# Softplus widths and last additions spread over GpSimd, scan begun with two decays

## The chip, the cores and the metric

The kernel runs on one core of a Trainium2 chip. The metric is device time in microseconds for one execution, inputs and outputs in HBM. One core has TensorE (PE, matmuls into PSUM), VectorE (DVE), ScalarE (ACT), GpSimd (POOL) and SyncE (SP, here a DMA queue). Each runs its own instruction list in order; they meet through semaphores. GpSimd cannot reach PSUM.

## The reference

A network of four blocks on an image `[2, 32, 32, 32]`: each block adds a mixer and then a token network to `x`. Only the first mixer, `L0_conv`, a windowed selective scan, is touched. Cut to what matters:

```python
def _forward(x, ...):                        # B=2, C=32, D=64, 16 states, 4 scan orders, windows 8x8
    xv, z = split(x @ in_proj_w.T)
    xc = silu(depthwise_conv3x3(xv) + conv_b)
    xs = four scan orders of the windows of xc            # Hilbert order, its transpose, both reversed
    dts, Bs, Cs = split(einsum('bkdl,kcd->bkcl', xs, x_proj_w))
    dts = softplus(einsum('bkrl,kdr->bkdl', dts, dt_projs_w) + dt_projs_b)
    A = -exp(A_logs)
    def step(h, (u, dt, Bl, Cl)):
        h = h * exp(dt[..., None] * A) + (dt * u)[..., None] * Bl[:, :, None, :]
        return h, einsum('bkdn,bkn->bkd', h, Cl)
    ys = lax.scan(step, 0, ...)
    y = layernorm(ys + Ds * xs, summed over the four orders, back in image order)
    return (y * silu(z)) @ out_proj_w.T
```

`dt` is called `step` in the kernel and `dt * u` is called `drive`.

## The kernel before

The kernel is a list of blocks; a block begins when all engines have finished the one before. Four matter here.

**The block of tokens and sequences** (L350 to L409) turns the convolution's result into scan order, `seq` `[128, 2, 16, 128]`: 128 partitions hold direction and channel, then come order `k`, window and position, 2 x 2048 columns in all. VectorE and ScalarE copy it out of PSUM in turns.

**The softplus block** (L426 to L507) works on 8 chunks of 512 columns, `cols(i)`. TensorE makes the raw step width `p_d` (bank `i % 4`) and, for the first four chunks, the raw B and C rows `p_bc`. softplus(v) is log(1 + exp(-|v|)) + max(v, 0), made precise by what rounding lost of exp(-|v|) in 1 + exp(-|v|):

- ScalarE, per chunk: Abs (L446) into `ex`, Relu (L447) into `above`, Exp (L449), and for i < 4 the copy of `p_bc` to bf16 `part[0]` (L452). Then eight logarithms (L457) into `step` after a table load (L454), and a last table load (L458).
- VectorE, per chunk: "keep" (L466), (ex + 1) - 1 into `drive`; "lost" (L473), ex - drive; the addition of it to `above` (L481); for i < 4 the remainder of B and C, `rest` (L470), its bf16 cast `part[1]` (L476) and the second remainder `part[2]` (L484). Then, 1024 columns wide, step = step - ln_one + above (L495) four times and drive = step * seq (L489) twice.
- SP stacks the three parts under each other into `b_parts` and `c_parts` (96 rows) by 12 DMAs (L506), part by part, and the block ends when all have landed. GpSimd has nothing.
- TensorE streams 16 filler matmuls (`keep_streaming`, L95) after the first logarithm.

**The scan block** (L557 to L776) has 64 units `u`, each 1024 columns of one of 16 states; four groups of 16 units (`NS`), so group 0 is the first half of order k = 0. Per unit: TensorE spreads a B row over the partitions (L587, `p_bb`) and a C row (L593, `p_cb`); ScalarE makes the decays exp(step * A) (L658, `d_a`) and copies `p_cb` out (L664, `cb`); VectorE multiplies drive and B into `p_bb` (L711) and scans (L722, `hs`); GpSimd multiplies by C (L775, `hc`); TensorE sums over states (L562, `p_y`). In each fourth unit ("on GpSimd") B goes by way of L615, ScalarE's copy (L669) and GpSimd's product (L770) into `d_bu`, and the decays into `p_bb`. Buffers are rings of three (`RING`): VectorE's scan of unit u waits for `hc` of unit u - 3, GpSimd's `hc` of unit u for TensorE's sum of u - 3, and on TensorE the sum of u - 3 stands ahead of the spread for u + 1. GpSimd also makes drive = step * seq for order k = 1 in units 2 and 18 (L766).

**The tail** of the scan block normalises, gates and mixes (up to L757). After it come the other blocks of the network, which the change does not touch.

Of the kernel before, what the change touches and what calls it, by code (L numbers as in the profile page):

```python
# [17 lines left out]
R = NB * C  # L18
# [41 lines left out]
def build_program(nc, io):  # L60
    with ExitStack() as ctx:
# [153 lines left out]
        with ExitStack() as st:  # L215
# [15 lines left out]
            pick = sb("pick", [96, NS, 128], BF16, stack=st)  # L231
            tok = sb("tok", [L, NW, D], stack=st)
# [3 lines left out]
            with ExitStack() as s2:  # L236
# [13 lines left out]
                with ExitStack() as s3:  # L250
# [10 lines left out]
                    with nc.Block() as block:  # L261
# [11 lines left out]
                        def _(pool):  # L273
                            pool.memset(padded[:], 0.0).then_inc(sig["border_zero"], 1)
                            pool.memset(w_dt[:], 0.0)
                            pool.wait_ge(sig["load_in"], 64)
# [65 lines left out]
                with ExitStack() as s3:  # L342
# [4 lines left out]
                    ln_one = sb("ln_one", [128, 2], stack=s2)  # L347
                    with nc.Block() as block:
                        @block.gpsimd
                        def _(pool):  # L350

                            pool.tensor_copy(pick[:], pick_f)
                            pool.memset(ln_one[:], 0.0)
# [51 lines left out]
                        @block.scalar  # L405
                        def _(act):
                            for i in range(1, NPAIR, 2):
                                act.wait_ge(sig["seq_made"], i + 1)
                                copy_seq(i, act.copy).then_inc(sig["seq_copied_odd"], 1)  # L409


                with ExitStack() as s3:
                    p_bc = ps("p_bc", [128, 4, BANK], stack=s3)
                    p_d = ps("p_d", [128, 4, BANK], stack=s3)
                    part = [sb(f"part{i}", [128, NW * L], BF16, stack=s3) for i in range(3)]
                    rest = sb("rest", [128, NW * L], stack=s3)
                    above = sb("above", [128, 2, NW * L], stack=s3)
# [4 lines left out]
                    def wide(m):  # L422
                        return m // 2, slice((m % 2) * 2 * BANK, (m % 2 + 1) * 2 * BANK)
                    seqf = seq[:].rearrange("p k w l -> p k (w l)")
                    with nc.Block() as block:
                        @block.tensor  # L426
                        def _(pe):
                            for i in range(NCH):
                                k, c = cols(i)
                                if i >= 4:  # L430
                                    pe.wait_ge(sig["step_read"], i - 3)
# [5 lines left out]
                            pe.wait_ge(sig["log1"], 1)  # L437
                            keep_streaming(pe, p_d[:, 0], 16)

                        @block.scalar  # L440
                        def _(act):
                            act.activation(ln_one[:, 1:2], ln_one[:, 1:2], ACT.Exp)
                            for i in range(NCH):
# [3 lines left out]
                                act.activation(above[:, k, c], p_d[:, i % 4], ACT.Relu, bias=b_dt[:, k:k + 1]).then_inc(sig["step_read"], 1)  # L447
                                act.wait_ge(sig["abs"], i + 1)
                                act.activation(ex[:, k, c], ex[:, k, c], ACT.Exp, scale=-1.0).then_inc(sig["exp_neg"], 1)  # L449
                                if i < 4:  # L450
                                    act.wait_ge(sig["bc_made"], i + 1)
                                    act.activation(part[0][:, c], p_bc[:, i], ACT.Copy).then_inc(sig["part_hi"], 1)  # L452
                            act.wait_ge(sig["exp_neg"], NCH)
                            act.activation(ln_one[:, 0:1], ln_one[:, 0:1], ACT.Ln, bias=1.0)  # L454
# [2053 lines left out]
```

## Time and profile before

| | |
|---|---|
| median of 3 runs | 994.14 us (993.59 to 1001.52) |
| profiled execution | 993.03 us |
| its span in the trace | 991.2 us |
| softplus block, 36.6 to 67.4 | 30.8 us |
| scan block up to the tail, 67.4 to 277.0 | 209.6 us |
| tail, 277.0 to 294.7 | 17.7 us |
| the rest, after 294.7 | 696.5 us |

The span runs from the first to the last instruction of the trace; the 1.8 us beyond it are in the execution's time but not in the trace. A row of the timeline gives start, duration, engine, line, operation, output and input with their shapes, count, and in brackets how long the engine had been idle and what ended that. Rows of a merged group give the time from its first start to its last end.

### The profile page before, as it was taken

The page shows a single profiled execution, that of the slowest core. Times are in us where ns is not written, and L with a number is a line of the kernel's source. Part 1 is how long each engine was busy: PE and PEld are TensorE (multiplying, and loading weights), DVE is VectorE, ACT ScalarE, POOL GpSimd, SP SyncE. Part 2 cuts the span into 40 slices and gives each one's busy share as a digit, 9 for nine tenths or more (in the row PEclk, how much of TensorE's full clock was granted, in tenths as well). Part 3 has the DMA queues.
Part 4 walks back from the last instruction along what each step waited for, and adds up shares of the span by engine and source line. Part 5 has one row for each costly group of instructions (what it writes and reads, how often), then busy time and mean ns, then how long its engine had stood idle before and what let it go on. Part 6 is the DMA issues. An engine that isn't in the chain of part 4 may idle for free. (4 is left out here: it accounts for less than half of the span.)

```text
span 991.2 us, 15215 instructions
## 1 busy us (share of the span) xinstructions
PE 893.9 (90%) x6134; PEld 514.5 (52%) x6134; DVE 418.7 (42%) x715; ACT 450.7 (45%) x1491; POOL 230.5 (23%) x140
## 2 busy tenths in 40 slices
PE   7848888888986877999999999999999999999986
PEld 4416767767753443344444444445555544554543
DVE  4599999999965554600000000002004500202763
ACT  4667777777635533243333333333333333334642
POOL 3209999899830000020000000000000000000410
PEclk9978999999996588799999999999999999999987
DMA  3020000000000001110000000000000000000000
GB/s 80 15 50 1 1 1 2 1 1 1 1 3 4 1 1 33 46 36 1 2 1 1 1 1 2 1 1 1 1 1 1 1 1 1 1 1 2 1 24 11
DMA packets 10319, 8.28 MB, mean 8 GB/s; under 512 B 7346, under 2 KB 8610, under 8 KB 10152
## 3 DMA queue, kind: packets, MB, share of 16 engines
q1 hardware_dynamic: 10248, 7.31, 2.9%
q8 instruction: 48, 0.79, 0.3%
q14 instruction: 23, 0.19, 0.1%
HBM read 5.47 MB, written 0.26 MB: 6 GB/s over the span
## 5 line engine op out<-in xcount | busy, mean ns | idle before, releaser
L890 PE MATMUL L2p_z<-stream 128*128 128x512 bf16 x943 | 366.7, 390 | 0.0
L932 ACT ACTIVATE L2yx<-L2p_z 32x2 f32<-32x2 f32 x1024 | 165.0, 161 | 323.3 <-PE L2p_z L909 323.2
L909 PEld LDWEIGHTS L2p_z<-L2yx,L2v 64*32 64x32 f32 x2048 | 137.6, 104 | 224.7 <-ACT L2yx L932 218.5
L909 PE MATMUL L2p_z<-L2yx,L2v 64*32 64x2 f32 x2048 | 225.5, 178 | 1.0 <-PEq L810 0.9
L775 POOL TENSOR_TENSOR hc<-hs,cb 128x1024 f32<-128x1024 f32 x64 | 149.5, 2358 | 10.7 <-DVE hs L722 10.7
L562 PEld LDWEIGHTS p_y<-ident,hc 128*128 128x128 f32 x1024 | 125.7, 194 | 10.8 <-POOL hc L775 1.5
L1588 DVE COPY xn<-L2yx 32x512 f32<-32x512 f32 (+1 forms) x2 | 0.8, 384 | 302.7 <-ACT L2yx L932 302.7
L562 PE MATMUL p_y<-ident,hc 128*128 128x128 f32 x1024 | 126.3, 277 | 0.3 <-POOL hc L775 0.3
L1588 POOL COPY xn<-L2yx 32x128 f32<-32x128 f32 x1 | 0.3, 283 | 484.2 <-SPq L1931 484.2
L722 DVE TENSOR_TENSOR_SCAN hs<-d_a,p_bb 128x1024 f32<-128x1024 f32 x48 | 109.7, 2286 | 6.8 <-ACT d_a L658 0.8
L890 PEld LDWEIGHTS L2p_z<-stream 128*128 128x128 bf16 x943 | 90.1, 96 | 15.1
L664 ACT ACTIVATE cb<-p_cb 128x1024 f32<-128x1024 f32 x64 | 65.2, 1019 | 13.0 <-PE p_cb L593 12.1
L658 ACT ACTIVATE d_a<-step,decay 128x1016 f32<-128x1016 f32 x48 | 54.6, 1138 | 18.5 <-DVE hs L722 11.6
L711 DVE TENSOR_TENSOR p_bb<-drive,p_bb 128x1024 f32<-128x1024 f32 x48 | 58.0, 1209 | 2.7 <-PE p_bb L587 2.6
L593 PE MATMUL p_cb<-c_parts,pick 96*128 96x512 bf16 x128 | 40.4, 399 | 12.3 <-ACT d_bu L669 10.5
L587 PE MATMUL p_bb<-b_parts,pick 96*128 96x512 bf16 x96 | 30.5, 400 | 12.7 <-DVE hs L722 6.3
L770 POOL TENSOR_TENSOR d_bu<-drive,d_bu 128x1024 f32<-128x1024 f32 x16 | 37.9, 2369 | 10.2 <-ACT d_bu L669 10.2
L982 PE MATMUL L0p_z<-L0yx,L0v 64*32 64x64 f32 x192 | 30.4, 306 | 10.0 <-PEq L810 4.5
L722 DVE TENSOR_TENSOR_SCAN hs<-p_bb,d_bu 128x1024 f32<-128x1024 f32 x16 | 36.3, 2266 | 0.7 <-ACT p_bb L658 0.7
L982 PEld LDWEIGHTS L0p_z<-L0yx,L0v 64*32 64x32 f32 x192 | 17.5, 139 | 22.5 <-ACT L0yx L1002 16.2
L593 PEld LDWEIGHTS p_cb<-c_parts,pick 96*128 96x128 bf16 x128 | 10.9, 99 | 31.3 <-ACT d_bu L669 18.8
L1002 ACT ACTIVATE L0yx<-L0p_z 32x64 f32<-32x64 f32 x96 | 20.1, 214 | 13.3 <-PE L0p_z L982 12.9
(509 smaller groups left out, 849.5 us busy)
## 6 DMA issues: line engine op xcount, KB each, us to landing
y_l<-in_pick SPq DMA_DIRECT2D x1, 768.0 KB
b_parts<-part SPq DMA_DIRECT2D x6, 128.0 KB, 2.3
c_parts<-part SPq DMA_DIRECT2D x6, 128.0 KB, 2.3
pos<-in_pos SPq DMA_DIRECT2D x1, 512.0 KB, 3.6
ao<-in_at_o SPq DMA_DIRECT2D x1, 512.0 KB, 3.9
L1w<-in_L_w SPq DMA_DIRECT2D x1, 297.0 KB
L3w<-in_L_w SPq DMA_DIRECT2D x1, 297.0 KB
x_tok<-in_x SPq DMA_DIRECT2D x2, 128.0 KB, 3.0
```

The costliest lines, as they stand in the source:

```text
L562: last = pe.matmul(p_y[:, j], hc[:, v % RING, j * L:(j + 1) * L], ident[:], start=False, stop=(v % NS == NS - 1 and j % 4 == 3))
L593: last = pe.matmul(p_cb[:, h * BANK:(h + 1) * BANK], pick[:, n], c_parts[:, k, c], start=True, stop=True)
L658: act.activation(dst[:, :, 1:L], src[:, :, 1:L], ACT.Exp, scale=decay[:, k, n:n + 1]).then_inc(sig["d_a"], 1)
L664: act.activation(cb[:, u % RING], p_cb[:], ACT.Copy).then_inc(sig["p_cb_read"], 1)
L711: dve.tensor_tensor(p_bb[:, u % 2], drive[:, k, c0:c0 + UC], p_bb[:, u % 2], ALU.mult).then_inc(sig["d_bu"], 1)
L722: dve.tensor_tensor_scan(hs[:, u % RING], decays, inputs, 0.0, ALU.mult, ALU.add).then_inc(sig["scanned"], 1)
L770: pool.tensor_tensor(d_bu_of(u), drive[:, k, c0:c0 + UC], d_bu_of(u), ALU.mult).then_inc(sig["d_bu_pool"], 1)
L775: pool.tensor_tensor(hc[:, u % RING], hs[:, u % RING], cb[:, u % RING], ALU.mult).then_inc(sig["hc"], 1)
L890: pe.matmul(p_z[:, 1, 0:each], stream[:, 0:128], stream[:, 0:each], start=True, stop=True)
L909: pe.matmul(p_step[:, t % 2], v[:, 0:C], yx[:, NB * t:NB * (t + 1)], start=True, stop=True).then_inc(s("preact"), 1)
L932: act.activation(yx[0:C, NB * (t + 1):NB * (t + 2)], p_step[:, t % 2], ACT.Sigmoid).then_inc(s("state"), 1)
L982: pe.matmul(p_z[0:C, f, 0:NB * n], v[:, 0:C], by_batch[:, cols], start=True, stop=True).then_inc(s("preact"), 1)
```

## The change

- Four buffers, `part`, `above`, `ln_one` (now three columns) and a constant `one`, live through the scan; `y_tok` and `y_sq` reuse `conv` and `tok`.
- The logarithm of one, its negative and a first exponential move to ScalarE's list in the block of tokens and sequences.
- Softplus block: VectorE makes max(v, 0) of chunks 0 to 3, by TENSOR_SCALAR from PSUM; ScalarE keeps Relu for chunks 4 to 7. "Keep" becomes a SCALAR_TENSOR_TENSOR with a broadcast column. `part[1]` comes straight from `p_bc` by a second subtraction, not by a cast. "Lost" (8) and `part[2]` (4) and the additions of chunks 4 to 7 go to GpSimd; VectorE keeps the additions of chunks 0 to 3, with ln_one in them. Only the first 1024 columns are finished in this block (one addition, one product).
- The other three quarters are finished in the scan block: the second by VectorE's addition ahead of unit 0 and GpSimd's product in unit 0; the third and fourth by ScalarE's subtraction of ln_one in units 2 and 18, GpSimd's addition in units 4 and 20 and its product in units 6 and 22 (before: 2 and 18).
- The parts are stacked by 18 DMAs in three pieces; TensorE waits for each at units 0, 16 and 32, and the softplus block no longer waits for their landing.
- 26 filler matmuls instead of 16, from the last exponential on, and 4 in each of units 0 to 2.
- ScalarE makes the decays of units 0 and 1 ahead of its first copy.

```diff
                         def _(pe):
                             for i in range(NCH):
                                 if i >= 4:
-                                    pe.wait_ge(sig["step_read"], i - 3)
+                                    pe.wait_ge(sig["abs"], i - 3)
+                                    pe.wait_ge(sig["positive_early"], i - 3)
...
-                            pe.wait_ge(sig["log1"], 1)
-                            keep_streaming(pe, p_d[:, 0], 16)
+                            pe.wait_ge(sig["exp_neg"], NCH)
+                            keep_streaming(pe, p_d[:, 0], 26)
...
                         @block.vector
                         def _(dve):
...
+                            def keep(i):
+                                k, c = cols(i)
+                                dve.wait_ge(sig["exp_neg"], i + 1)
+                                dve.scalar_tensor_tensor(drive[:, k, c], ex[:, k, c], 1.0, one[:].broadcast_to([128, BANK]), ALU.add, ALU.subtract).then_inc(sig["kept"], 1)
+
+                            def add_lost(i):
+                                k, c = cols(i)
+                                dve.wait_ge(sig["lost"], i + 1)
+                                dve.scalar_tensor_tensor(above[:, k, c], above[:, k, c], ln_one[:, 0:1], drive[:, k, c], ALU.subtract, ALU.add).then_inc(sig["with_max"], 1)
+
+                            for i in range(4):
+                                k, c = cols(i)
+                                dve.wait_ge(sig["abs"], i + 1)
+                                dve.tensor_scalar(above[:, k, c], p_d[:, i], b_dt[:, k:k + 1], 0.0, ALU.add, ALU.max).then_inc(sig["positive_early"], 1)
+                                if i:
+                                    keep(i - 1)
+                                dve.wait_ge(sig["part_hi"], i + 1)
+                                dve.tensor_tensor(part[1][:, c], p_bc[:, i], part[0][:, c], ALU.subtract)
+                                dve.tensor_tensor(rest[:, c], p_bc[:, i], part[0][:, c], ALU.subtract).then_inc(sig["rest"], 1)
+                                if i >= 2:
+                                    dve.wait_ge(sig["positive_early"], i - 1)
+                                    add_lost(i - 2)
+                            for i in range(3, NCH):
+                                keep(i)
+                                if i < 5:
+                                    add_lost(i - 1)
...
+                            dve.tensor_tensor(step[:, k, c], step[:, k, c], above[:, k, c], ALU.add).then_inc(sig["softplus"], 1)
+                            dve.wait_ge(sig["softplus"], 1)
+                            dve.tensor_tensor(drive[:, k, c], step[:, k, c], seqf[:, k, c], ALU.mult)
+
+                        @block.gpsimd
+                        def _(pool):
+                            for i in range(NCH):
+                                k, c = cols(i)
+                                pool.wait_ge(sig["kept"], i + 1)
+                                pool.tensor_tensor(drive[:, k, c], ex[:, k, c], drive[:, k, c], ALU.subtract).then_inc(sig["lost"], 1)
+                                if i < 4:
+                                    pool.wait_ge(sig["rest"], i + 1)
+                                    pool.tensor_tensor(part[2][:, c], rest[:, c], part[1][:, c], ALU.subtract).then_inc(sig["part_lo"], 1)
+                                else:
+                                    pool.wait_ge(sig["lost"], i + 1)
+                                    pool.tensor_tensor(above[:, k, c], above[:, k, c], drive[:, k, c], ALU.add)
...
+                            stack("parts_of_0", 2, 0, slice(0, 2 * BANK))
+                            stack("parts_of_1", 4, 0, slice(2 * BANK, 4 * BANK))
+                            stack("parts_of_2", 4, 1, slice(0, 4 * BANK))
...
+                                if u < RING:
+                                    keep_streaming(pe, p_y[:, 0:4].rearrange("p w d -> p (w d)"), 4)
...
+                            if u == 0:
+                                decays(0)
+                                decays(1)
+                            elif u >= 2:
+                                decays(u)
...
+                            if u in (2, 2 + NS):
+                                c = slice(u // NS * UC, (u // NS + 1) * UC)
+                                act.activation(step[:, 1, c], step[:, 1, c], ACT.Identity, bias=ln_one[:, 2:3]).then_inc(sig["late_log"], 1)
...
+                        second = slice(UC, 2 * UC)
+                        dve.tensor_tensor(step[:, 0, second], step[:, 0, second], above[:, 0, second], ALU.add).then_inc(sig["softplus"], 1)
...
-                            if u in (2, 2 + NS):
-                                c = slice(u // NS * UC, (u // NS + 1) * UC)
+                            if u == 0:
+                                c = slice(UC, 2 * UC)
+                                pool.wait_ge(sig["softplus"], 2)
+                                pool.tensor_tensor(drive[:, 0, c], step[:, 0, c], seqf[:, 0, c], ALU.mult)
+                            c = slice(u // NS * UC, (u // NS + 1) * UC)
+                            if u in (4, 4 + NS):
+                                pool.wait_ge(sig["late_log"], u // NS + 1)
+                                pool.tensor_tensor(step[:, 1, c], step[:, 1, c], above[:, 1, c], ALU.add).then_inc(sig["late_step"], 1)
+                            if u in (6, 6 + NS):
+                                pool.wait_ge(sig["late_step"], u // NS + 1)
                                 pool.tensor_tensor(drive[:, 1, c], step[:, 1, c], seqf[:, 1, c], ALU.mult)
```

## Rows read from the trace of the kernel before

**Rows 1.** The page: busy time, share of the span and instructions of each engine.
```profile
PE 893.9 (90%) x6134; PEld 514.5 (52%) x6134; DVE 418.7 (42%) x715; ACT 450.7 (45%) x1491; POOL 230.5 (23%) x140
```

**Rows 2.** Windows by stage: length, busy of PE, PEld, DVE, ACT, POOL; clock; DMA.
```profile
36.60:67.40 30.80, 17.52 (x48) 5.41 (x48) 26.14 (x42) 23.96 (x42) 0.00 (x0) 0.87 0.23 52
67.40:277.00 209.60, 184.32 (x1296) 145.91 (x1297) 199.64 (x113) 153.65 (x169) 188.64 (x82) 0.96 0.00 1
294.70:991.20 696.50, 650.33 (x4461) 335.67 (x4461) 166.63 (x517) 254.84 (x1247) 26.63 (x32) 0.93 0.02 6
```

**Rows 3.** Timeline of the softplus block: first and last of TensorE and ScalarE.
```profile
36.64 1.10 PE L432 MATMUL p_d<-seq,w_dt 128*128 128x512 f32 x2 [0.94 <-PEq L348]
38.68 1.12 PE L432 MATMUL p_d<-seq,w_dt 128*128 128x512 f32 x2
38.01 0.67 ACT L446 ACTIVATE ex<-p_d,b_dt 128x512 f32<-128x512 f32 x1
59.13 1.28 ACT L458 ACT_TABLE_LOAD   x1
```

**Rows 4.** Groups of instructions: line, engine, shapes, count | busy us, mean ns | idle.
```profile
L466 DVE TENSOR_SCALAR drive<-ex 128x512 f32<-128x512 f32 x8 | 3.4, 420 | 5.2 <-ACT ex L449 5.2
L470 DVE TENSOR_TENSOR rest<-p_bc,part 128x512 f32<-128x512 f32 x4 | 2.7, 681 | 0.0
L489 DVE TENSOR_TENSOR drive<-step,seq 128x1024 f32<-128x1024 f32 x2 | 2.4, 1218 | 0.0
```

**Rows 5.** GpSimd alone, groups with shapes kept apart.
```profile
L775 POOL TENSOR_TENSOR hc<-hs,cb 128x1024 f32<-128x1024 f32 x64 | 149.5, 2358 | 10.7 <-DVE hs L722 10.7
L355 POOL TENSOR_TENSOR skip<-skip 128x128 f32<-128x128 f32 x1 | 0.4, 449 | 0.0
```

**Rows 6.** Attention stage: timeline rows, and durations min/median/max of two lines.
```profile
L1555 DVE TENSOR_TENSOR scored<-scored,anmx x8: 1224/1225/2782, 749.6 to 927.5; 128x1024 f32<-128x1024 f32 x8
927.50 2.78 DVE L1555 TENSOR_TENSOR scored<-scored,anmx 128x1024 f32<-128x1024 f32 x1
942.04 1.26 DVE L2094 SCALAR_TENSOR_TENSOR sc<-sc,pos 128x128 f32<-128x128 f32 x1
925.38 3.82 POOL L2267 TENSOR_TENSOR prod<-e 128x1024 f32<-128x1024 f32 x2 [9.84 <-DVE e L1786]
L2273 POOL TENSOR_TENSOR prod<-e x8: 293/298/1279, 929.2 to 931.9; 128x64 f32<-128x64 f32 x8
940.30 2.85 POOL L2280 TENSOR_TENSOR pv<-sc,e 128x1024 f32<-128x1024 f32 x1 [2.35 <-ACT sc L2221]
```

**Rows 7.** Timeline of the start of the scan block: GpSimd, then VectorE.
```profile
67.41 0.12 POOL L762 MEMSET d_a<- 128x16 f32 x1 [35.89 <-POOLq L425]
68.49 1.23 DVE L711 TENSOR_TENSOR p_bb<-drive,p_bb 128x1024 f32<-128x1024 f32 x1 [1.37 <-PE p_bb L587]
72.35 1.23 DVE L711 TENSOR_TENSOR p_bb<-drive,p_bb 128x1024 f32<-128x1024 f32 x1 [0.24 <-PE p_bb L587]
79.40 2.26 DVE L722 TENSOR_TENSOR_SCAN hs<-p_bb,d_bu 128x1024 f32<-128x1024 f32 x1
```

**Rows 8.** Timeline of VectorE: two scans of the on-GpSimd kind, units 11 and 15.
```profile
105.14 2.26 DVE L722 TENSOR_TENSOR_SCAN hs<-p_bb,d_bu 128x1024 f32<-128x1024 f32 x1
117.95 2.26 DVE L722 TENSOR_TENSOR_SCAN hs<-p_bb,d_bu 128x1024 f32<-128x1024 f32 x1
```

**Rows 9.** Timeline of GpSimd in the scan: its first pauses.
```profile
105.30 4.68 POOL L775 TENSOR_TENSOR hc<-hs,cb 128x1024 f32<-128x1024 f32 x2 [0.23 <-DVE hs L722]
118.11 4.68 POOL L775 TENSOR_TENSOR hc<-hs,cb 128x1024 f32<-128x1024 f32 x2 [1.16 <-DVE hs L722]
```

**Rows 10.** Windows of 2 us, columns as in Rows 2; TensorE's clock after POOL.
```profile
53.00:55.00 2.00, 0.00 (x0) 0.00 (x0) 1.97 (x5) 1.97 (x4) 0.00 (x0) 0.50 0.32 74
59.00:61.00 2.00, 2.00 (x9) 0.71 (x7) 1.96 (x3) 1.60 (x3) 0.00 (x0) 0.86 0.15 33
77.00:79.00 2.00, 2.00 (x7) 1.08 (x7) 1.90 (x2) 1.95 (x2) 2.00 (x2) 0.50 0.00 0
```

More of the change, by code:

```diff
@@ L231, in build_program @@
             pick = sb("pick", [96, NS, 128], BF16, stack=st)
+            part = [sb(f"part{i}", [128, NW * L], BF16, stack=st) for i in range(3)]
+            above = sb("above", [128, 2, NW * L], stack=st)
+            ln_one = sb("ln_one", [128, 3], stack=st)
+            one = sb("one", [128, 1], stack=st)
             tok = sb("tok", [L, NW, D], stack=st)
@@ L275, in _ @@
                             pool.memset(w_dt[:], 0.0)
+                            pool.memset(ln_one[:], 0.0)
+                            pool.memset(one[:], 1.0)
                             pool.wait_ge(sig["load_in"], 64)
@@ L452, in _ @@
                                     act.activation(part[0][:, c], p_bc[:, i], ACT.Copy).then_inc(sig["part_hi"], 1)
+                                else:
+                                    act.activation(above[:, k, c], p_d[:, i % 4], ACT.Relu, bias=b_dt[:, k:k + 1])
+                                act.wait_ge(sig["abs"], i + 1)
+                                act.activation(ex[:, k, c], ex[:, k, c], ACT.Exp, scale=-1.0).then_inc(sig["exp_neg"], 1)
                             act.wait_ge(sig["exp_neg"], NCH)
-                            act.activation(ln_one[:, 0:1], ln_one[:, 0:1], ACT.Ln, bias=1.0)
                             for i in range(NCH):
@@ L500, in _, with stack @@
                         @block.sync
                         def _(sp):
-                            for i, s in enumerate(("part_hi", "part_mid", "part_lo")):
-                                sp.wait_ge(sig[s], 4)
-                                for k in range(2):
+                            def stack(name, chunks, k, c):
+                                for i, s in enumerate(("part_hi", "rest", "part_lo")):
+                                    sp.wait_ge(sig[s], chunks)
                                     for dst, row in ((b_parts, 0), (c_parts, 32)):
-                                        sp.dma_start(dst[32 * i:32 * i + 32, k], part[i][k * R + row:k * R + row + 32]).then_inc(sig["parts_stacked"], 16)
@@ L645, in read_y, with decays @@
                             act.copy(group_out(g, 0, HW8), group_in(0, HW8)).then_inc(sig["y_read"], 1)
-                        act.wait_ge(sig["first_decay_zero"], 1)
-                        for u in range(NU):
+                        def decays(u):
                             k, c0, n = unit(u)
+                            if u == NS:
+                                act.wait_ge(sig["softplus"], 2)
+                            if u in (2 * NS, 3 * NS):
+                                act.wait_ge(sig["late_step"], u // NS - 1)
                             if u >= 2:
@@ L696, in _ @@
                         for i, w in enumerate((0, 4)):
[L697 to L698 removed]
+                            act.wait_ge(sig["y_summed"], NU + i)
+                            act.copy(group_out(3, w, 4), group_in(w, 4)).then_inc(sig["y_read"], 1)
                         squares(1)
```

70 lines of the change are left out of this document (18 added, 52 removed).

## The prediction

> **What bounds the kernel now.** I read the page's busy times first [rows 1]: TensorE leads with 90%, but that is a sum over stages and partly filler, so it says little about this change. The table by stage [rows 2] shows where the edits live: a softplus stage of 30.8 us (36.60 to 67.40), the scan of 209.6 us, 17.7 us of tail, and 696.5 us in which no line is touched. Within the stages I then read the timeline.
>
> *Softplus stage.* ScalarE's chunk work begins at 38.01 and its last table load at 59.13 [rows 3]; the next block begins only at 67.41 [rows 7]. In between only VectorE works (26.14 of 30.8 us busy, with a late start); GpSimd does nothing (0.00) [rows 2]. VectorE ends the stage.
>
> *Scan stage.* VectorE is busy 199.64 of 209.6 us, GpSimd 188.64, ScalarE 153.65 [rows 2]. Per four units VectorE needs three products and four scans: 3 x 3.54 + 2.20 = 12.8 us, what lies between two scans of the on-GpSimd kind [rows 8]. GpSimd needs four `hc` and one `d_bu` at a spacing of 2.33 us (two in 4.68) = 11.7 us [rows 9]. So VectorE sets the scan, with GpSimd 1.1 us behind it per four units. GpSimd is the one to watch: its first pause once started, of 0.23 us, comes at 105.30, 37.9 us into the block, and only at 118.11 does it show the steady gap of 1.16 us [rows 9].
>
> **The change, part by part.**
>
> *Start of the stage.* The first table load (1.28) and a 0.20 exponential move to the block before, where ScalarE has idle time. But the first `p_d` matmul ends at 37.74 and Abs began at 38.01 [rows 3]: 0.2 us won, no more.
>
> *ScalarE.* Four Relu go to VectorE. TensorE's repeat of `p_d` and `p_bc` is 2.06 us (36.64, 38.68) [rows 3], so three ScalarE passes per chunk (about 1.6 us) now wait for it, where four took as long as TensorE. Exponentials end near 52.7 instead of 53.4, logarithms near 58.4, the last table load near 59.7. ScalarE alone would end the block near 60.
>
> *VectorE.* 8 keeps grow from 0.42 (TENSOR_SCALAR) to about 0.69 (two-input form); 4 positives (0.69), 8 part differences (0.68) and 4 additions (0.69) are its own; then one 1024-wide addition and one product (1.22 each) [rows 4]. That is 24 passes at a spacing near 0.61 plus 2.4: about 17 us from 38.5, done near 57 if nobody holds it up.
>
> *GpSimd* gets 16 passes of 128x512. No such shape is in the trace: 128x128 takes 449 ns, 128x1024 takes 2358 [rows 5]; so on a line between them 1.27, a spacing of 1.24 like the 2.33 for 2.36. The first can start when the first keep is done: Abs, copy and Exp of chunk 0 end near 39.95, the second positive is ahead of the keep on VectorE, so near 42.0. Sixteen passes: 42.0 + 19.8 = 61.8, a few waits for keeps: 62.3. Other 1024-wide forms give bounds: 3.82 for two, and 2.85 [rows 6]; half of each is 0.96 and 1.42, so 15.3 to 22.7 us for the sixteen.
>
> *The port.* Whether these passes run beside VectorE's decides the case. In the attention stage a VectorE TENSOR_TENSOR of 1024 with both inputs in SBUF takes 1.22 seven times and 2.78 once (min and median against max) [rows 6]. The long one began at 927.50 while GpSimd's second product (3.82 for two from 925.38) ran until 929.20; 929.2 - 927.5 + 1.2 is 2.9. Of GpSimd's next eight passes, from 929.2, one took 1279 ns where the others took 298 [rows 6]: it waited for VectorE. Once more: a SCALAR_TENSOR_TENSOR of only 128 columns at 942.04 took 1.26, and ended 0.15 us behind the GpSimd pass of 2.85 that had begun at 940.30 [rows 6]. The scans do not show it: one of their two inputs is in PSUM. So I take it that a VectorE pass with two SBUF inputs and a GpSimd pass exclude each other wholly.
> The Trainium skill, "SBUF — State Buffer", section "Who interferes with whom", says this of just these operand kinds, and that `tensor_scalar` in its fast form excludes GpSimd too, so that the new form of the keep would free nothing. By that rule the sum is the same 999; without it, rival B's. The trace agrees for the two-input passes (2.78 against 1.22) and shows no fast form beside GpSimd.
>
> After 42.0 VectorE has 7 keeps and 4 additions (11 x 0.65 = 7.2) and two wide passes (2.4) with both inputs in SBUF. These 9.6 us do not fit under GpSimd's 19.8: 42.0 + 19.8 + 7.2 + 2.4 = 71.4. In the long pass above the pair overlapped by about 0.14, so some of it comes back; waits for keeps cost some. I take 71.0 for the end, 71.3 for the next block, against 67.41: **+3.9 us**. With the bounds of the GpSimd pass: +0.4 to +6.8.
>
> *DMAs in pieces.* 18 issues on SP's queue replace 12; I put one at 0.6 us, and twice that would change nothing. Pieces of the first half need `part_lo` of two chunks (near 48.4), the last eight follow the fourth near 56.7, landing near 64. Only unit 0's pieces must be there at 71.3: nothing. If the port is no obstacle, the fourth is at 52.3 and all has landed near 60, still ahead of 62.6.
>
> *Clock.* TensorE falls to 0.5 (1.2 GHz) once idle since 48.6, is back at full (2.4 GHz) near 59.5, when filler had run since 55.5, and is still at 0.5 at 77 to 79 after idling from 61 to 67 [rows 10]. 26 fillers instead of 16, from 52.7: ten at 0.43 and sixteen at 0.21, done near 60.4. With 11 us idle behind them the scan again begins at 1.2 GHz.
>
> *Scan start* (relative to the block's start; before: products 0 and 1 at 1.08 and 4.94, scan 3 at 11.99 [rows 7]). VectorE first adds for 1.22: product 0 at 1.35, scan 0 at 2.7. On TensorE four fillers (1.7 at this clock) stand ahead of unit 3's B spread, and ScalarE's copy comes after two decays: that spread starts at 3.6 instead of 3.0, product 1 at 5.5, scan 1 at 6.85. Again for unit 2 (fillers after the spread of unit 1): scan 2 near 10.7, scan 3 near 12.95. So 0.95 later.
>
> *GpSimd in the scan.* Three more passes net: product in unit 0, additions in units 4 and 20; the products of 2 and 18 move to 6 and 22. Queued behind are `d_bu`, then all `hc`; VectorE waits for `hc` three units back, TensorE sums them ahead of the next B spread. Chained at 2.33: unit 7's `hc` ends at 34.1 after the start (before, 30.7), unit 8's at 38.7, exactly when scan 11 wants it, and the spread for unit 12 is 0.15 late. Once more after units 20 and 22. Together 0.3 us; the bound is both additions whole, 4.7. ScalarE's two subtractions (1.1 each) lie in its slack. The tail keeps its work; the reused buffers cost nothing.
>
> *Sum.* Profiled execution: 993.03 (span 991.2 and 1.8 around it); +3.9 + 0.95 + 0.15 = +5.0, so 998.0. The median of the runs is 994.14, 1.1 more: **999 us**.
>
> **Rivals.**
> *A. The port excludes, and lengths are as taken*: 999; own range 994.5 (short passes -3.5, scan start early -1.0) to 1003.5 (long ones +2.9 and waits +1.6, or the waits alone near their bound). Chance 0.70.
> *B. No exclusion for 512-wide passes.* GpSimd ends the block at 62.3, next block 62.6: -4.8, TensorE idle for only 2.2 us, so at full clock, scan start +0.2, ties +0.3: 994.1 - 4.3 = 990. For it: the scans' GpSimd spacing of 2.33 is unhurt by VectorE. Against it: the three long passes of [rows 6]. 0.10. This is the faster side; it decides as soon as VectorE's 9.6 us run beneath.
> *C. The gain and the loss cancel.* GpSimd passes as short as the 3.82-for-two form: +0.4 in place of +3.9, the rest as above: 995.5. Against it: that form reads other operands, and 82 passes of the plain one take 2.36. 0.10.
> *D. GpSimd becomes the bound of the scan.* If VectorE inherits all three added passes (7.0) on top of 3.9 and 0.95: 994.1 + 11.9 = 1006. For it: no pause before 105.30 already now [rows 9]. Against it: the slack of 1.1 per four units. It decides from 5 us of such waits on. 0.10.
>
> A run of this kernel tells about 1% (9.9 us) from no change. A and C lie within; B too. Slower: D and the edge of A, 0.11. Faster: B with a further gain, 0.03. Same: 0.86. The range leaves out B and D: 992 to 1004.
>
> **What would show it.** In the softplus stage GpSimd should be busy from 42 to 71 with mean passes well over 1.27, and VectorE's 512-wide two-SBUF passes between 0.69 and 1.9; PSUM-fed ones stay at 0.68. The scan block should start near 71.3 at clock 0.5. First scan 2.7 behind it; scan 11 to 12 with a gap under 0.5; scan spacing later unchanged. If GpSimd's passes stay at 1.27 with VectorE's at 0.69, B holds. If scans in units 8 to 15 are spaced over 3.6, D holds. I would be wrong outright if the later stages moved, 696.5 us that I take as fixed, for instance by the clock's falls coming elsewhere.

## The result, and the profile after

| | before | after |
|---|---|---|
| median | 994.43 us (20 runs, 990.52 to 1001.98) | 1000.15 us (20 runs, 997.03 to 1009.35) |
| ratio | | 1.0053, 95% interval 1.0037 to 1.0069 |
| profiled execution / span | 993.03 / 991.2 us | 1000.17 / 998.4 us |
| scan block begins at | 67.41 | 69.37 |
| last of the 64 scans begins at | 274.53 | 279.90 |
| next block begins at | 294.71 | 300.73 |

The changed kernel is slower by half a per cent, 5.3 us by the ratio. 999 us with no change beyond 1% was forecast. Of the 7.2 us between the two spans, 1.96 arise in the softplus block, 3.41 in the scan, 0.65 in the tail and 1.2 in blocks that the change does not touch. This is a sum over one profiled execution of each kernel; the 5.3 us are over 20 runs of each.

The busy times of the page, against [rows 1]: GpSimd has 32.1 us more, and VectorE has 1.9 more, not less.

```profile
PE 899.9 (90%) x6156; PEld 518.8 (52%) x6156; DVE 420.6 (42%) x700; ACT 451.8 (45%) x1491; POOL 262.6 (26%) x160
```

The same stages as in [rows 2], by window (length, then busy time of PE, PEld, DVE, ACT, POOL; clock; DMA):

```profile
36.60:69.36 32.76, 19.59 (x58) 6.19 (x58) 26.55 (x26) 20.78 (x35) 24.69 (x16) 0.85 0.21 49
69.36:282.00 212.64, 185.86 (x1304) 147.13 (x1305) 200.74 (x113) 154.76 (x171) 195.66 (x85) 0.97 0.00 1
282.00:300.70 18.70, 15.56 (x125) 9.99 (x123) 10.77 (x17) 4.85 (x10) 2.72 (x2) 0.91 0.00 1
300.70:998.40 697.70, 650.75 (x4461) 336.96 (x4461) 166.62 (x517) 254.81 (x1247) 26.63 (x32) 0.93 0.02 6
```

VectorE's busy time in the softplus stage did not shrink (26.55 against 26.14), though it does 26 passes where it did 42. GpSimd is busy for 24.69 us with 16 passes: 1.54 each.

The groups of that stage, VectorE's against [rows 4] (in each: line, engine, operation, shapes, count, busy us, mean ns, idle time before):

```profile
L505 POOL TENSOR_TENSOR drive<-ex,drive 128x512 f32<-128x512 f32 x8 | 12.5, 1558 | 12.4 <-DVE drive L470 12.4
L511 POOL TENSOR_TENSOR above<-above,drive 128x512 f32<-128x512 f32 x4 | 6.6, 1645 | 0.3
L508 POOL TENSOR_TENSOR part<-rest,part 128x512 bf16<-128x512 f32 x4 | 6.0, 1497 | 0.0
L470 DVE SCALAR_TENSOR_TENSOR drive<-ex,one 128x512 f32<-128x512 f32 x8 | 11.4, 1445 | 0.0
L484 DVE TENSOR_TENSOR part<-p_bc,part 128x512 bf16<-128x512 f32 x4 | 2.7, 682 | 0.2 <-ACT part L454 0.2
L496 DVE TENSOR_TENSOR step<-step,above 128x1024 f32<-128x1024 f32 x1 | 2.3, 2278 | 0.0
```

Read them by their inputs. `part[1]` from `p_bc` (L484, one input in PSUM) takes the 682 ns it took before. The keeps (L470, two inputs in SBUF) take 1445 ns where 690 was expected of the form, the wide addition (L496) 2278 where its like took 1218. GpSimd's passes take 1.50 to 1.65 us. The timeline shows the turns:

```profile
58.73 1.72 POOL L505 TENSOR_TENSOR drive<-ex,drive 128x512 f32<-128x512 f32 x1
60.53 1.59 POOL L511 TENSOR_TENSOR above<-above,drive 128x512 f32<-128x512 f32 x1
60.92 2.28 DVE L496 TENSOR_TENSOR step<-step,above 128x1024 f32<-128x1024 f32 x1
62.08 2.24 POOL L505 TENSOR_TENSOR drive<-ex,drive 128x512 f32<-128x512 f32 x1
67.81 1.26 POOL L511 TENSOR_TENSOR above<-above,drive 128x512 f32<-128x512 f32 x1
69.37 0.12 POOL L797 MEMSET d_a<- 128x16 f32 x1 [0.29 <-POOLq L430]
```

GpSimd's additions and losses (58.73, 60.53, 62.08) start 1.55 to 1.80 us apart, each just as a VectorE pass gives way; the addition of 1.22 us that VectorE began at 60.92 lasts 2.28. In this stretch GpSimd goes at 1.26 only when VectorE has nothing left (before, it did so beside VectorE's PSUM-fed passes: the losses begun at 42.19, 45.22 and 48.69 took 1.27 to 1.28), and its last pass ends at 69.07, which lets the scan block begin at 69.37 ([rows 7]: 67.41). VectorE had then been idle for 4.0 us.

In the scan, the start is as good as before [rows 7]: scan 0, 1 and 3 at 2.51, 6.15 and 11.86 us after the block's start, against 2.42, 6.27 and 11.99. Scans 0 and 3 on VectorE's timeline:

```profile
71.88 2.29 DVE L757 TENSOR_TENSOR_SCAN hs<-d_a,p_bb 128x1024 f32<-128x1024 f32 x1
81.23 2.26 DVE L757 TENSOR_TENSOR_SCAN hs<-p_bb,d_bu 128x1024 f32<-128x1024 f32 x1
```

The reason is in the windows of 1 us (clock after POOL):

```profile
72.00:73.00 1.00, 1.00 (x4) 0.32 (x3) 1.00 (x1) 0.61 (x1) 1.00 (x1) 0.50 0.00 0
73.00:74.00 1.00, 1.00 (x4) 0.24 (x2) 1.00 (x1) 0.25 (x1) 0.07 (x1) 0.77 0.00 0
74.00:75.00 1.00, 0.32 (x2) 0.11 (x2) 0.98 (x2) 0.78 (x1) 0.15 (x1) 1.00 0.00 0
```

TensorE's clock goes from 0.5 to full between 73 and 74, about 4 us after the block's start; before, it was still at 0.5 ten to twelve us after it [rows 10].

The loss comes at units 11 and 12, where two scans were 2.20 and 3.52 behind the one before and are now 2.85 and 5.47. First the timeline:

```profile
105.08 9.26 POOL L818 TENSOR_TENSOR hc<-hs,cb 128x1024 f32<-128x1024 f32 x4
107.46 3.68 PE L577 MATMUL p_y<-ident,hc 128*128 128x128 f32 x16 [1.84 <-POOL hc L818]
107.50 2.29 DVE L757 TENSOR_TENSOR_SCAN hs<-p_bb,d_bu 128x1024 f32<-128x1024 f32 x1 [0.56 <-POOL hc L818]
111.61 1.23 DVE L746 TENSOR_TENSOR p_bb<-drive,p_bb 128x1024 f32<-128x1024 f32 x1 [1.83 <-PE p_bb L604]
112.97 2.29 DVE L757 TENSOR_TENSOR_SCAN hs<-d_a,p_bb 128x1024 f32<-128x1024 f32 x1
```

and the same stretch in windows of 2 us:

```profile
105.00:107.00 2.00, 0.63 (x4) 0.12 (x3) 1.93 (x1) 0.57 (x1) 2.00 (x2) 1.00 0.00 0
107.00:109.00 2.00, 1.54 (x7) 1.54 (x8) 1.50 (x1) 1.50 (x2) 2.00 (x2) 0.65 0.04 8
109.00:111.00 2.00, 2.00 (x12) 1.94 (x11) 0.79 (x1) 0.56 (x1) 2.00 (x2) 0.50 0.00 0
```

GpSimd is in an unbroken run of `hc` (105.08). TensorE waits 1.84 us for unit 8's, and scan 11 (107.50) waits 0.56. TensorE's sum then takes 3.68 us; such a sum of 16 records takes 1.95 elsewhere. The three windows show why: the clock fell to 0.5 at about 107.6 (0.65 is the mean of 107 to 109), after a wait in which TensorE was busy for 0.63 of 2 us. B for unit 12 stands behind that sum, so VectorE's product waits 1.83 more. The same happens, smaller, at units 27 to 29 (0.22 + 1.30 + 0.53 us): in all, scans 11, 12 and 27 to 29 come 4.65 us late (0.65 + 1.95 + 2.05).

The tail's 0.65 us are not the change's. From the last scan to VectorE's first pass of the next block this execution took 21.34 us and the one of before 20.69; but the narrow GpSimd, PSUM-input, old-keep and filler-less runs below, which have the changed kernel's tail, took 20.69 too. In this execution the clock fell once more, at about 295.7 (window of 1 us, clock after POOL):

```profile
295.00:296.00 1.00, 0.97 (x22) 0.98 (x24) 0.57 (x1) 0.00 (x0) 0.00 (x0) 0.67 0.00 0
```

### The profile page after: what moved, and what is told of

It reads as the page before. It is cut to its first block and busy times, and to the rows that moved or that the text cites. A ratio compares the mean times of both kernels' runs of the same rounds, so it can differ in the third digit from the quotient of the medians.

```text
span 998.4 us, 15272 instructions
## 1 busy us (share of the span) xinstructions
PE 899.9 (90%) x6156; PEld 518.8 (52%) x6156; DVE 420.6 (42%) x700; ACT 451.8 (45%) x1491; POOL 262.6 (26%) x160
## 3 DMA queue, kind: packets, MB, share of 16 engines
HBM read 5.47 MB, written 0.26 MB: 6 GB/s over the span
## 5 line engine op out<-in xcount | busy, mean ns | idle before, releaser
L680 ACT ACTIVATE d_a<-step,decay 128x1016 f32<-128x1016 f32 x48 | 54.5, 1137 | 15.6 <-POOL d_a L797 9.5
L1045 ACT ACTIVATE L0yx<-L0p_z 32x64 f32<-32x64 f32 x96 | 20.1, 214 | 13.3 <-PE L0p_z L1025 13.0
```

Of the source, the lines that this page charges most:

```text
L680: act.activation(dst[:, :, 1:L], src[:, :, 1:L], ACT.Exp, scale=decay[:, k, n:n + 1]).then_inc(sig["d_a"], 1)
```

## Experiments

Every experiment but one starts from the changed kernel. "Block start" is when the scan block begins (after: 69.37), "last scan" how long after it the 64th scan begins (after: 210.53; before: 207.12).

### GpSimd's passes made narrow

```diff
-    pool.tensor_tensor(drive[:, k, c], ex[:, k, c], drive[:, k, c], ALU.subtract)
+    pool.tensor_tensor(drive[:, k, few], ex[:, k, few], drive[:, k, few], ALU.subtract)
```

`few`, written here for short, is the first 8 columns of `c`; the third part and the addition to `above` are cut in the same way.

> The changed kernel with all 16 GpSimd passes of the softplus block cut from 512 to 8 columns (the losses, the third part and four additions are left out but for 8 columns, so steps and parts are not the reference's; a memset of the third part is added in the block before). Theory (VectorE passes with two SBUF inputs and GpSimd passes exclude each other, and GpSimd's 16 set the block's end): the keeps fall from a mean of 1.45 us to 0.69, VectorE is through near 58, ScalarE's last table load sets the end and the scan block starts near 60.4 instead of 69.37. Rival (VectorE's passes are long for another reason, such as ScalarE or the DMAs): keeps stay above 1 us and the block starts at 64 or later.

VectorE's group of keeps:

```profile
L471 DVE SCALAR_TENSOR_TENSOR drive<-ex,one 128x512 f32<-128x512 f32 x8 | 5.3, 684 | 0.0
```

and the fillers on TensorE's timeline:

```profile
52.96 8.05 PE L95 MATMUL p_d<-stream 128*128 128x512 bf16 x26 [4.33 <-ACT ex L459]
```

The keeps are back at 684 ns, and the wide addition, 2278 in the changed kernel, at 1226; VectorE was through at 58.0. Block start 61.27, 8.1 us earlier (expected 60.4), one run 987.73 us. What holds the last 1.3 us is neither ScalarE (done at 60.0) nor VectorE but the 26 fillers, which end at 61.01. I had them done near 60.4; in the changed kernel they ended at 60.47, 8.6 us ahead of GpSimd.

### VectorE's two-input passes made narrow

```diff
-    dve.scalar_tensor_tensor(drive[:, k, c], ex[:, k, c], 1.0, one[:].broadcast_to([128, BANK]), ALU.add, ALU.subtract)
+    dve.scalar_tensor_tensor(drive[:, k, few], ex[:, k, few], 1.0, one[:].broadcast_to([128, 8]), ALU.add, ALU.subtract)
```

`add_lost` is cut in the same way.

> The changed kernel with VectorE's 8 keeps and 4 additions cut from 512 to 8 columns (the correction of softplus is left out but for 8 columns; a memset of drive is added in the block before); the two 1024-wide passes stay. Theory (exclusion): GpSimd's passes fall from a mean of 1.56 to 1.28 us, 42.1 + 16 x 1.26 = 62.3, and 2.3 for the two wide VectorE passes: last GpSimd pass ends near 64.5, the scan block starts near 64.8. Rival (512-wide GpSimd passes take 1.5 us or more by themselves): the start stays at 69.

Block start 63.71 (expected 64.8). 0.6 us of the difference is that GpSimd's first pass began at 41.52 where I had 42.1. Its `part[2]` passes take 1161 ns where they took 1497; its losses 1398 (1558) and additions 1484 (1645), with the two wide VectorE passes still in the way of one loss (2.27 us) and one addition (2.13). A GpSimd pass of 512 columns is thus 1.16 to 1.27 us by itself. One run took 994.47 us.

### Same width, but one input from PSUM

```diff
-    dve.scalar_tensor_tensor(drive[:, k, c], ex[:, k, c], 1.0, one[:].broadcast_to([128, BANK]), ALU.add, ALU.subtract)
+    dve.scalar_tensor_tensor(drive[:, k, c], p_bc[:, i % 4], 0.0, one[:].broadcast_to([128, BANK]), ALU.mult, ALU.mult)
-    dve.scalar_tensor_tensor(above[:, k, c], above[:, k, c], ln_one[:, 0:1], drive[:, k, c], ALU.subtract, ALU.add)
+    dve.scalar_tensor_tensor(above[:, k, c], p_bc[:, i % 4], 0.0, drive[:, k, c], ALU.mult, ALU.add)
```

> The changed kernel with one input of every keep and of the four additions taken from PSUM (p_bc, times 0) in place of SBUF, all passes still 512 wide; keep is then zero and the steps are not the reference's. Theory (it is the second SBUF input that excludes): the keeps fall from 1.45 to about 0.69 us although as wide as before, GpSimd's passes to about 1.28, and the scan block starts near 64.8 (only the two wide passes still collide). Rival (any VectorE pass collides with GpSimd, whatever it reads): nothing changes, start near 69.4.

The groups of GpSimd, then of VectorE:

```profile
L505 POOL TENSOR_TENSOR drive<-ex,drive 128x512 f32<-128x512 f32 x8 | 11.2, 1394 | 11.3 <-DVE drive L470 11.2
L508 POOL TENSOR_TENSOR part<-rest,part 128x512 bf16<-128x512 f32 x4 | 4.6, 1160 | 0.0
L470 DVE SCALAR_TENSOR_TENSOR drive<-p_bc,one 128x512 f32<-128x512 f32 x8 | 5.3, 680 | 0.0
L475 DVE SCALAR_TENSOR_TENSOR above<-p_bc,drive 128x512 f32<-128x512 f32 x4 | 2.7, 682 | 0.2 <-POOL drive L505 0.2
L496 DVE TENSOR_TENSOR step<-step,above 128x1024 f32<-128x1024 f32 x1 | 1.8, 1791 | 1.7 <-ACT step L462 1.7
```

and the first pass of the scan block on the timeline:

```profile
64.80 0.13 POOL L797 MEMSET d_a<- 128x16 f32 x1 [0.29 <-POOLq L430]
```

Nothing is narrower here and no pass is gone. Still the keeps take 680 ns, the additions 682 (986), GpSimd's third part 1160. L496, left with both inputs in SBUF, still takes 1791. Block start 64.80, as expected to the digit. So for these two-input passes it is the second SBUF input that shuts out GpSimd; width and number of the passes did not change, only what they read and compute. On the 12 passes it costs 4.6 us. One run took 992.69 us.

The run also had the wait at unit 11 (unit 8's `hc` comes just after scan 11 wants it), and shows it without the fall of the clock, on the timeline:

```profile
102.56 2.05 PE L577 MATMUL p_y<-ident,hc 128*128 128x128 f32 x16 [1.83 <-POOL hc L818]
102.60 2.29 DVE L757 TENSOR_TENSOR_SCAN hs<-p_bb,d_bu 128x1024 f32<-128x1024 f32 x1 [0.36 <-POOL hc L818]
```

and in a window, 1.00 after POOL:

```profile
102.00:104.00 2.00, 1.44 (x12) 1.44 (x13) 1.64 (x2) 1.40 (x2) 2.00 (x2) 1.00 0.04 8
```

TensorE waited 1.83 us here and 1.84 in the changed kernel, but at clock 1.00 the sum took 2.05 against 3.68, and scan 12 came 3.85 behind scan 11 instead of 5.47. The wait itself cost 0.8 us in these two gaps (0.45 + 0.33; the changed kernel had 0.2 more at scan 11), the clock 1.6. The narrow GpSimd run also had 3.85, the narrow VectorE run 5.48, the run below 5.49: such a wait is followed by the fall in some executions and not in others, and what decides it stays open. With units 27 to 29 the loss was 1.2 and 1.3 us in the narrow GpSimd run and this one, whose clock stayed up, and 3.1, 4.6 and 4.65 in the run below, the narrow VectorE run and the changed kernel.

### The keep in its old form

```diff
-    dve.scalar_tensor_tensor(drive[:, k, c], ex[:, k, c], 1.0, one[:].broadcast_to([128, BANK]), ALU.add, ALU.subtract)
+    dve.tensor_scalar(drive[:, k, c], ex[:, k, c], 1.0, -1.0, ALU.add, ALU.add)
```

> The changed kernel with the keep in its old form, TENSOR_SCALAR (0.42 us alone) in place of SCALAR_TENSOR_TENSOR (0.69). Theory 1 (by the Trainium skill, SBUF - State Buffer, Who interferes with whom, the fast form of tensor_scalar excludes GpSimd too): keeps still wait and last up to 1.5 us, but each holds the port for about 0.3 less: 7 x 0.3 = 2.1, scan block starts near 67.3. Theory 2 (a one-input pass runs beside GpSimd): keeps last 0.42, 7 x 0.58 = 4.1 less, the block starts near 65.3.

VectorE's group of keeps:

```profile
L470 DVE TENSOR_SCALAR drive<-ex 128x512 f32<-128x512 f32 x8 | 9.3, 1181 | 0.0
```

and the block start on the timeline:

```profile
67.13 0.12 POOL L797 MEMSET d_a<- 128x16 f32 x1 [0.29 <-POOLq L430]
```

The keeps still wait: mean 1181 ns for a form that takes 420 alone. Block start 67.13, where 67.3 was expected with the exclusion and 65.3 without. So the one-input TENSOR_SCALAR, from SBUF to SBUF, shuts GpSimd out as well, and the wider form that the change gave the keep cost 2.2 us and bought nothing. The Trainium skill, "SBUF — State Buffer", section "Who interferes with whom", says that `tensor_scalar` can take both port pairs and so contend with GpSimd; by that rule this run starts late, and it did (1181 against 420 ns). The same section says that the blocked engine waits for the whole instruction of the other; here the measurement differs a little: in the changed kernel an excluded pair of 1.27 and 0.68 took 1.68 us, as worked out below. One run took 995.13 us.

### The late passes elsewhere in the scan

```diff
-    if u in (4, 4 + NS):
+    if u in (12, 12 + NS):
...
-    if u in (6, 6 + NS):
+    if u in (20, 20 + NS):
```

The first pair holds GpSimd's addition to `step`, the second its product into `drive`; the product's columns and its wait are set back by one group, so that units 20 and 36 finish the halves that units 6 and 22 did.

> The changed kernel, computing the same, with GpSimd's two late additions moved from units 4 and 20 to 12 and 28, and its late products from 6 and 22 to 20 and 36. Theory (the additions and products come while GpSimd is still behind from the scan's start, so scans 11, 12, 27, 28 and 29 wait, 0.65 + 1.95 + 0.22 + 1.30 + 0.53 = 4.65 us in the changed kernel's profile): these gaps close to 2.20, 3.52 and 3.54 and the last scan starts at 205.9 after the block's start instead of 210.53; the median falls by 4 to 5 us to about 995.5. Rival (GpSimd has no room for the passes wherever they stand): the waits move to units 13 to 20 and 29 to 36, the last scan starts at 209 or later.

Scans 11 and 12 on VectorE's timeline:

```profile
106.73 2.26 DVE L757 TENSOR_TENSOR_SCAN hs<-p_bb,d_bu 128x1024 f32<-128x1024 f32 x1
110.25 2.29 DVE L757 TENSOR_TENSOR_SCAN hs<-d_a,p_bb 128x1024 f32<-128x1024 f32 x1
```

3.52 behind each other. Last scan 206.08 (expected 205.9), with only 0.17 lost before scan 20 (and 0.36 at scan 40, as in the changed kernel). Median 996.6 us of 10 runs (expected 995.5), 1.0011 of before (0.9984 to 1.0038): 3.5 us under the changed kernel, and not to be told from before. The same passes fit once GpSimd has caught up.

### The late additions left out

```diff
-    pool.tensor_tensor(step[:, 1, c], step[:, 1, c], above[:, 1, c], ALU.add)
+    pool.tensor_tensor(step[:, 1, few], step[:, 1, few], above[:, 1, few], ALU.add)
```

> The changed kernel with GpSimd's two late additions cut to 8 of 1024 columns at their old places (the steps of the last two quarters lack max(v, 0) but for 8 columns). Theory: with 2.3 us less in GpSimd's queue before units 11 and 27 no scan waits for it, last scan at 205.9 to 206.5 after the block's start. Rival (the wait comes from unit 0's product or from the late products): scans 11 and 12 still wait 0.5 us or more between them.

Last scan 206.19, no wait at 11, 12 or 27 to 29. Together with the run before this puts the scan's loss at these units on the additions of units 4 and 20; unit 0's product and the products of 6 and 22 alone do no harm. The time (1003.62) is of no use: this execution's opening block ran 5.3 us longer, see the last section.

### Without the fillers of units 0 to 2

```diff
-    if u < RING:
-        keep_streaming(pe, p_y[:, 0:4].rearrange("p w d -> p (w d)"), 4)
```

> The changed kernel without the 12 filler matmuls of units 0 to 2. Theory (in the changed kernel they bring TensorE to full clock at 73 where before it came at 79.5, which is why the scan's start lost nothing): the granted clock stays at 0.5 until 78 or later, scan 1 starts 6.4 to 6.6 us after the block's start instead of 6.15, scan 3 at 12.1 to 12.4 instead of 11.86. Rival (as I predicted, the fillers only stand in the way): clock the same as with them, scan 3 at 11.8 or sooner.

A window late in the start, its clock after POOL:

```profile
78.00:80.00 2.00, 0.26 (x1) 0.13 (x2) 1.90 (x3) 2.00 (x4) 2.00 (x2) 0.50 0.00 0
```

and product 4 and scan 4 on VectorE's timeline:

```profile
84.95 1.23 DVE L744 TENSOR_TENSOR p_bb<-drive,p_bb 128x1024 f32<-128x1024 f32 x1 [1.25 <-PE p_bb L604]
86.31 2.29 DVE L755 TENSOR_TENSOR_SCAN hs<-d_a,p_bb 128x1024 f32<-128x1024 f32 x1
```

The clock is still 0.5 at 78 to 80, where with fillers it was 1.00 from 74. Scan 1 at 6.55, scan 3 at 12.27, and scan 4 came 4.87 behind it (a wait of 1.25 for TensorE): 1.76 us later than with fillers by unit 4. Without them nothing came sooner, and the clock was full only at about 83.7. But the last scan came at 208.14, 2.4 us sooner than in the changed kernel: with scan 11 1.76 us later, unit 8's `hc` was there for it, and scans 11 and 12 came without a wait (2.21, 3.51). TensorE itself still waited 1.84 us for that `hc`, but here its clock stayed up, and units 27 to 29 lost 0.55 us. A start won on VectorE's side only brought it earlier to the engine that was behind. One run took 999.51 us.

### The scan's start alone, on the kernel before

```diff
+    if u < RING:
+        keep_streaming(pe, p_y[:, 0:4].rearrange("p w d -> p (w d)"), 4)
...
+    if u == 0:
+        decays(0)
+        decays(1)
+    elif u >= 2:
+        decays(u)
```

> The kernel before, computing the same, with two parts of the change alone: ScalarE's decays of units 0 and 1 first, and four filler matmuls in units 0 to 2. VectorE's addition ahead of unit 0 and GpSimd's product are not in it. Theory (the fillers bring the clock up about 4 us after the block's start): scan 1 starts 6.0 to 6.2 us after the block's start instead of 6.27, scan 4 15.3 to 15.4 instead of 15.63, and full clock is granted by 73 instead of 79.5. Rival (my prediction: fillers and decays stand in the way at 1.2 GHz): scan 1 at 6.8, scan 3 at 12.9.

Scan 1 at 5.93, scan 4 at 15.17 (15.63), clock 0.82 over 70 to 72 and 1.0 from 72: all a little sooner than expected. That is 0.46 us won by unit 4, by the fillers and the early decays together. At scan 8 1.26 us were lost (4.78 instead of 3.52): GpSimd, with the product of unit 2, was behind, TensorE waited 1.80 us for its `hc`, and the clock fell at about 91. The last scan came at 206.94 against 207.12 only because this execution did not have the fall of the clock at 182 that the one of before has. One run 995.46 us.

### Half of GpSimd's softplus work back on VectorE

```diff
-    for i in range(3, NCH):
-        keep(i)
+    for i in range(3, NCH + 2):
+        if i < NCH:
+            keep(i)
+        if 5 <= i <= NCH:
+            lost_here(i - 1)
+        if i >= 6:
+            add_here(i - 2)
```

`lost_here` and `add_here` are the losses and additions of chunks 4 to 7, as TENSOR_TENSOR on VectorE; GpSimd's loop runs over chunks 0 to 3 alone. The keep is the old TENSOR_SCALAR, and the late passes stand in units 12, 20, 28 and 36.

> Computes the same. The changed kernel with the losses and additions of chunks 4 to 7 back on VectorE (8 GpSimd passes of 1.25 us become 8 of 0.61 that nothing has to take turns with), the keep in its old form, and the late passes spaced as in s1_spaced. Theory: GpSimd is done near 54, VectorE ends the softplus block near 62.5 with ScalarE's last table load at 60 just under it; scan block starts near 62.8 (after: 69.37), last scan 205.9 behind it; median about 1000.15 - 6.6 - 4.65 = 989, ratio to before 0.995. Rival (work on VectorE counts as much as on GpSimd): the block starts at 66 or later.

GpSimd's last pass of the stage and the first of the next, on the timeline:

```profile
52.82 1.33 POOL L522 TENSOR_TENSOR part<-rest,part 128x512 bf16<-128x512 f32 x1
63.18 0.13 POOL L808 MEMSET d_a<- 128x16 f32 x1 [9.03 <-POOLq L430]
```

GpSimd ends at 54.15; VectorE, then alone, at 62.92. Block start 63.18 (expected 62.8), 6.2 us under the changed kernel and 4.2 under the kernel before. Median 988.54 us of 5 runs (986.96 to 989.96), ratio to before 0.9928 (0.9898 to 0.9957), where the changed kernel has 1.0053 (1.0037 to 1.0069): small, but faster than both. Last scan 207.34 (expected 205.9): waits of 1.07 before scan 16 and 0.76 before scan 20 were left, the first with the clock fallen.

### The same with the late passes in other units

```diff
-    if u in (12, 12 + NS):
+    if u in (10, 10 + NS):
...
-    if u in (20, 20 + NS):
+    if u in (22, 22 + NS):
```

> Computes the same. As v1_vector_takes_half (988.54 us, last scan 207.34 after the block's start, waits of 1.07 before scan 16 and 0.76 before scan 20), with the late additions in units 10 and 26 and the products in 22 and 38, so that no addition stands directly ahead of a fourth unit's B product. Theory: the two waits vanish and nothing takes their place, last scan at 205.7 to 206.1, block start still 63.2, median 986.5 to 988. Rival (unit 10 is too early, GpSimd is still behind from the start): waits of 0.5 us or more at scans 11 to 13, and the median is 988.5 or more.

Both waits vanished (last scan 206.11 although unit 1 waited 0.5 at clock 0.5), as expected. The median did not follow (986.5 to 988 expected): 989.71 us of 12 runs (986.82 to 993.69), ratio 0.9948 (0.9921 to 0.9975), against 988.54; the two cannot be told apart. In its profile, span 991.6, the part behind 417, which the edits do not touch, takes 574.7 us where v1's takes 566.9 behind 419.9. A gain of one us in the scan is less than that part moves by itself.

## Why the prediction was right, and where it was not

*The port.* Right, and the reason for the softplus stage's loss. It was read from a VectorE pass of 2.78 us and two more long passes, one of each engine [rows 6]; the PSUM-input run shows it with width and number of the passes unchanged. VectorE and GpSimd took turns until VectorE was out of work.

*The softplus stage, +3.9: measured +1.96.* The mis-sized term is the turn. I added spacings, 1.24 + 0.65 = 1.89 us for a GpSimd and a VectorE pass, and gave back 0.4 us in all for the overlap of 0.14 that [rows 6] showed. The overlap comes at every change of hands: the losses of chunks 4 and 5 begin at 55.38 and 58.73, two turns, 1.68 each. Eleven turns x 0.2 = 2.2 us, and the end is 69.07, not 71.0. The overlap belonged in the sum at every turn; at the two wide passes too (62.08 to 66.48 is 4.40 us for what sums to 4.9). That each turn gives back the same is an estimate from these few. Keeps of up to 1.75 us, PSUM-fed passes at 0.68: as listed under what would show it. One bound was added up wrongly: sixteen passes in 15.3 us instead of 19.8 give 4.5 us less, not 3.5, so the lower bound of the term was -0.6 and not +0.4, and rival C stood at 994.5.

*ScalarE, DMAs, the moved table loads.* All hidden, as costed: Abs began at 37.92 (38.01), the last table load at 58.58, stacking DMAs were issued by 60.4. The logarithms' earlier end bought nothing.

*The clock at the scan's start.* Right that it begins at 0.5 (0.50 from 64 on). Wrong that the fillers only stand in the way: they brought the clock up at 73.5 and the 0.95 us that I charged was -0.13 at scan 3, -0.25 at scan 4. The filler-less run shows that it is the fillers (1.76 us by scan 4); the run on the kernel before agrees (0.46 us), but has the early decays too. It is not so in every execution: in the last two variants the clock was full at the block's start, fell 5 and 1 us into it with the fillers in place, and was full again only after 8 to 9 us.

*GpSimd in the scan, 0.15 to 0.3: measured 4.65.* The chain was placed well: unit 8's `hc` came 38.1 us after the block's start, 38.7 was forecast "exactly when scan 11 wants it". But VectorE was on time where I had it 0.95 late, so the tie became a wait; and behind it TensorE's clock could fall, which nearly doubled the time of the sum (3.68 us) and more than doubled the cost (1.6 of 2.6 us at units 11 and 12). Where it did not fall, the same late passes lost 1.2 and 1.3 us in all, so the wait was missed by about one us and the rest of the 4.65 is the clock, for which the sum had no term. The run with spaced passes takes it all back. The net, +3.41, is 4.65 and 0.36 more at unit 40, less 0.25 at the start, less 1.35 us that the profiled execution of before lost at units 33 to 37: 0.36 at scan 33, at full clock, and 0.98 at scans 36 and 37, behind a fall of its own clock at 182. Rival D named this mechanism but priced it by three whole passes; what counts is how late GpSimd is, and what a late sum does to the clock. Of D's signs one came true: scan 12 was 5.47 us behind scan 11, over the 3.6 named, though the scans of units 13 to 15 were not; and 4.65 us is close to the 5 from which D was to decide.

*The sum.* +5.0 forecast, +7.2 in the spans, +5.3 by the ratio. The median was met to 1.2 us, but partly by luck, since errors with opposite signs helped: 1.9 us too much in the softplus stage and 1.2 at the scan's start, about 4.5 too little for GpSimd's waits in the profiled execution. The 0.65 us of the tail and the 1.2 behind it were taken as nothing, and rightly as far as the change goes. Of the 1.2: a stretch of one untouched block takes either 13.3 us (before, the old keep, the spaced passes, both last variants) or 15.3 to 15.6 us (after and the other runs, the one with two small edits to the kernel before among them), whatever the edit; other untouched stretches took 0.9 of these 2.1 us back.

*Rivals.* B (no exclusion) fell: it needed keeps of 0.69. C fell too: GpSimd's short form was not the one at work, though the stage ended between C and A.

## What to carry to other kernels

Before work goes from VectorE to GpSimd, look at the inputs of what VectorE does meanwhile: beside passes fed from PSUM GpSimd is free, beside two-input SBUF passes (or a TENSOR_SCALAR from SBUF) every pass of either adds to the sum, and GpSimd's are twice as long. Give it as many passes as VectorE has PSUM-fed ones to cover them, no more. And put extra passes of an engine that runs close behind the leading one where it has caught up, not where the code first allows them: a wait that idles TensorE can cost its clock as well. Before a gap of one or two us between two single profiles is put down to an edit, look in the other profiles for the same gap in blocks that no edit touches.

## What the runs showed of the hardware

The exclusion overlaps by about 0.2 us at each change of hands, so two excluded passes of 1.27 and 0.68 take 1.68 together, not 1.95 (or 1.89 by spacings). TENSOR_SCALAR of one SBUF input excludes GpSimd too (1181 against 420 ns).

A wait of TensorE of 1.84 us was followed by half the clock in the changed kernel, and one of 1.83 us by full clock in the PSUM-input run: 3.68 and 2.05 us for the same sum. Of six executions with this wait at unit 8's `hc`, 1.83 to 1.85 us each, the clock fell in three (changed kernel, narrow VectorE, old keep) and stayed in three (narrow GpSimd, PSUM input, no fillers). Four fillers in each of units 0 to 2 had the clock up 4 us after the block's start in the changed kernel; without them it was still at half after 14.

TensorE can run at half speed in the opening block. In the run with the additions left out its f32 matmuls from 11.9 to nearly 25 are slow, while VectorE's and ScalarE's passes are not: the same two records of `p_z` take 1.91 us instead of 1.02, though the clock is given as 1.00 in both; all that follows is 5.3 us later. First the changed kernel, then that run:

```profile
15.39 1.02 PE L295 MATMUL p_z<-xn,w_in 64*128 64x512 f32 x2
```

```profile
17.33 1.91 PE L295 MATMUL p_z<-xn,w_in 64*128 64x512 f32 x2
```

That this also makes the runs of 999 to 1002 us among those of before is likely, but no profile of such a run was at hand.
